# Fourth layer of a cross-attention kernel: scores in halves, two transpose banks, K and Q projected two blocks ahead

## The reference, cut to what matters

```
Q = x Wq' + bq,  K = ctx Wk' + bk,  V = ctx Wv' + bv          (256 -> 256, 16 heads of 16)
A = softmax(Q K' / 4)  per head                               (128 x 128, no mask)
y = x + (A V) Wo' + bo
out = (y - mean) / sqrt(var + 1e-5) * gamma + beta
```

## Time and profile before

| | |
|---|---|
| runs | 3356.8, 3352.99, 3349.3 us |
| profiled execution | 3355.26 us, its span 3353.6 us |
| TensorE (matmul) busy | 3019.1 us, 90% of the span |
| VectorE busy | 2043.1 us, 61% |
| ScalarE busy | 1894.9 us, 57% |
| POOL busy | 1487.5 us, 44% |
| mean granted TensorE clock | 0.959 of full speed |
| fourth layer | first exponentials at 3024 us, end at 3353.6 us |

### The profile page before, as it was taken

One profiled execution on the slowest core, in us unless ns is written; L12 is line 12 of the kernel. 1 busy time (PEld: TensorE's weight loads), 2 busy tenths in 40 slices (PEclk: granted clock), 3 DMA queues, 4 the chain that ended last, 5 costly groups with the idle time before them and its releaser, 6 DMA issues. The chain is left out here.

```text
span 3353.6 us, 82485 instructions
## 1 busy us (share of the span) xinstructions
PE 3019.1 (90%) x28656; PEld 2682.5 (80%) x28656; DVE 2043.1 (61%) x4340; ACT 1894.9 (57%) x7796; POOL 1487.5 (44%) x1874
## 2 busy tenths in 40 slices
PE   8999999689999999637999999999999999847886
PEld 6999998479999999636888888888888888746665
DVE  3445454244444444336777787788778877726775
ACT  3444444134444444326777777777777777616664
POOL 1233422103444544611555555555555555543545
PEclk9999999899999999868999999999999999978998
DMA  3112221311111110032222222333111111123331
GB/s 131 58 57 68 80 76 38 132 48 39 45 53 53 53 46 20 35 129 78 86 74 70 67 69 73 95 93 123 56 58 59 61 61 57 33 69 97 96 100 40
DMA packets 218390, 232.87 MB, mean 69 GB/s; under 512 B 41952, under 2 KB 183264, under 8 KB 215904
## 3 DMA queue, kind: packets, MB, share of 16 engines
q1 hardware_dynamic: 218208, 230.49, 21.6%
HBM read 148.57 MB, written 65.01 MB: 64 GB/s over the span
## 5 line engine op out<-in xcount | busy, mean ns | idle before, releaser
L1757 ACT ACTIVATE middle_stage<-middle_psum,middle_neg_max 128x128 f32<-128x128 f32 x2048 | 726.1, 391 | 330.4 <-DVE middle_neg_max L1737 330.2
L1757 ACT ACTIVATION_READ_ACCUMULATOR middle_stage<-middle_psum,middle_neg_max 128x1 f32 x2048 | 471.8, 230 | 0.0
L1737 DVE TENSOR_REDUCE middle_neg_max<-middle_psum 128x4 f32<-128x512 f32 x512 | 337.3, 680 | 51.2 <-PE middle_psum L1700 49.1
L1711 PE MATMUL middle_psum<-middle_eye,middle_stage 128*128 128x128 f32 x2048 | 321.5, 280 | 18.4 <-DVE middle_stage L1743 8.3
L1711 PEld LDWEIGHTS middle_psum<-middle_eye,middle_stage 128*128 128x128 f32 x2048 | 231.9, 142 | 71.8 <-issue 46.4
L1666 POOL TENSOR_TENSOR middle_attended_lo<-middle_mix,middle_attended_hi 128x256 fp32r<-128x256 f32 x128 | 94.9, 741 | 436.4 <-DVE middle_attended_hi L1749 436.4
L1757 ACT ACTIVATE fourth_stage<-fourth_psum,fourth_neg_max 128x128 f32<-128x128 f32 x512 | 182.9, 400 | 93.5 <-DVE fourth_neg_max L1737 93.4
L536 POOL TENSOR_TENSOR cross_ff_hidden_lo<-cross_ff_relu,cross_ff_hidden_hi 128x256 fp32r<-128x256 f32 x128 | 100.9, 789 | 279.7 <-DVE cross_ff_hidden_hi L531 279.7
L97 PE MATMUL middle_psum<-middle_n_yt_hi,middle_w_lo 128*128 128x256 f32 x640 | 194.1, 303 | 13.7 <-ACT middle_n_y L1874 12.1
L1967 POOL TENSOR_TENSOR middle_ff_hidden_lo<-middle_ff_relu,middle_ff_hidden_hi 128x256 fp32r<-128x256 f32 x256 | 183.5, 737 | 48.8 <-DVE middle_ff_hidden_hi L1961 48.8
L1743 DVE COPY middle_stage<-middle_psum 128x512 f32<-128x512 f32 x256 | 175.2, 684 | 16.8 <-PE middle_psum L1711 16.5
(11 more groups left out here) (351 smaller groups left out, 10910.4 us busy)
## 6 DMA issues: line engine op xcount, KB each, us to landing
middle_stage<-middle_a_k SPq DMA_DIRECT2D x1024, 16.0 KB, 1.8
middle_xt_hi<-x_hi SPq DMA_DIRECT2D x32, 256.0 KB, 2.7
middle_xt_lo<-x_lo SPq DMA_DIRECT2D x32, 256.0 KB, 3.0
middle_mask_flags<-flags SPq DMA_DIRECT2D x128, 64.0 KB, 1.9
middle_ct_hi<-context_hi SPq DMA_DIRECT2D x32, 256.0 KB, 2.9
middle_ct_lo<-context_lo SPq DMA_DIRECT2D x32, 256.0 KB, 3.1
middle_x_rows<-x_rows SPq DMA_DIRECT2D x32, 256.0 KB, 2.7
x_rows<-middle_n_z SPq DMA_DIRECT2D x32, 256.0 KB, 2.2
```

The source lines that it names most:

```text
L1711: ins = pe.transpose(banks.psum[:, TURN_BANK, x * SEQ:(x + 1) * SEQ], self.sh.p_wide[:, 4 * b + t, x, :], self.sh.eye[:])
L1737: dve.tensor_reduce(self.sh.neg_max[:, 4 * b + t, :], psum[:, SCORE_BANKS[t], :].rearrange("p (x k) -> p x k", x=4), AX_X, ALU.max, negate ...
L1757: ins = act.activation(self.sh.p_wide[:, 4 * b + t, x, :], psum[:, SCORE_BANKS[t], x * SEQ:(x + 1) * SEQ], ACT.Exp, bias=self.sh.neg_max[: ...
```

## The change

In the fourth layer alone:

- `AttendHalves` takes the place of `AttendWide`. `pe_scores` does one **half**, two of the four banks (0 and 1, or 2 and 3), and signals by itself; it claims only its two banks.
- The scores run half a step further ahead: step `here` makes scores (here,1, second half), (after,0, both halves) and (after,1, first half). The maxima move along.
- `pe_turn` and `dve_turned` alternate between banks 4 and 7; V goes through bank 6 with K, Q and the output projection.
- K and Q are both projected and evicted for block here+2. Q was projected for here+1 before. K comes at the start of the step, Q near its end.
- SP loads `x` for block here+4 behind the K copies and the residual rows, where it loaded it for here+3 ahead of them. Its store comes last, as before.
- Ahead of the loop, Q of block 1 and one and a half more scores calls are made.

POOL's order and the numbers of matmul, VectorE and ScalarE instructions per block stay the same. The diff, cut to its core:

```diff
+class AttendHalves(AttendWide):
+    visits = 2 * B2
+    turn_banks = (TURN_BANK, FF_BANK)
+    def pe_scores(self, pe, r, banks, b, half):
+        if b == 0 and half == 0:
...
+        tokens = slice(b * SEQ, (b + 1) * SEQ)
+        groups = (2 * half, 2 * half + 1)
+        banks.claim(pe, r, *(SCORE_BANKS[t] for t in groups))
+        for c in range(C):
+            for t in groups:
+                rows = slice(32 * t, 32 * t + 32)
+                ins = pe.matmul(banks.psum[:, SCORE_BANKS[t], c * T2:(c + 1) * T2].rearrange(
+                    "p (e k) -> p e k", e=2), self.proj.q[rows, c, tokens], self.proj.k_block[rows, c, :, tokens],
+                    start=True, stop=True)
+        ins.then_inc(self.scores_ready.sem, 1)
+        for t in groups:
+            banks.read(SCORE_BANKS[t], self.exp_done, 4 * b + t + 1, r=r)
+    def pe_turn(self, pe, r, banks, b, t):
+        bank = self.turn_banks[t % 2]
...
+    def dve_max(self, dve, r, psum, b, t):
+        dve.wait_ge(self.scores_ready.sem, self.scores_ready.at(r, 2 * b + t // 2 + 1))
...
 class Track:
-        self.proj = Project16(kit, f"a{i}", layer.weights_of(0), layer.stream, FF_BANK)
+        self.proj = Project16(kit, f"a{i}", layer.weights_of(0), layer.stream)
-        self.att = AttendWide(kit, f"a{i}", self.proj, [None], layer.out_of(0), layer.sh)
+        self.att = AttendHalves(kit, f"a{i}", self.proj, [None], layer.out_of(0), layer.sh)
...
 # sync, body
-                    if loaded:
-                        loaded[0].sp_x(sp, loaded[1], x, tokens(r, i, 3))
+                    queries = near(r, i, 4)
                     if keys:
                         keys[0].proj.sp_k_chunk(sp, keys[1], 0)
...
                         keys[0].sp_rows(sp, keys[1], x, tokens(r, i, 2))
+                    if queries:
+                        queries[0].sp_x(sp, queries[1], x, tokens(r, i, 4))
                     if before:
                         before[0].sp_store(sp, before[1], out, tokens(r, i, -2))
...
 # scalar, body
                     exp(here, 1, 0)
+                    exp(here, 1, 1)
+                    if keys:
+                        keys[0].proj.act_k(act, keys[1], psum)
                     if before:
                         before[0].att.act_spread(act, before[1], psum, 1)
-                    exp(here, 1, 1)
                     exp(here, 1, 2)
-                    if after:
-                        after[0].proj.act_q(act, after[1], psum)
                     exp(here, 1, 3)
                     exp(after, 0, 0)
-                    if keys:
-                        keys[0].proj.act_k(act, keys[1], psum)
                     exp(after, 0, 1)
                     if here:
                         here[0].att.act_spread(act, here[1], psum, 0)
                     exp(after, 0, 2)
+                    if keys:
+                        keys[0].proj.act_q(act, keys[1], psum)
                     exp(after, 0, 3)
...
 # vector, body, as it is after the change
                     inverse(here, 0)
                     maximum(here, 1, 2)
                     turned(here, 0, 0)
                     maximum(here, 1, 3)
                     turned(here, 0, 1)
                     norm(before, 1)
                     turned(here, 0, 2)
                     maximum(after, 0, 0)
                     maximum(after, 0, 1)
                     after[0].proj.dve_v(dve, after[1], psum)
                     turned(here, 0, 3)
                     inverse(here, 1)
                     maximum(after, 0, 2)
                     turned(here, 1, 0)
                     maximum(after, 0, 3)
                     before[0].norm.dve_sum(...)
                     turned(here, 1, 1)
                     norm(here, 0)
                     turned(here, 1, 2)
                     maximum(after, 1, 0)
                     maximum(after, 1, 1)
                     before[0].norm.dve_moments(dve, before[1])
                     turned(here, 1, 3)
...
 # tensor, body, as it is after the change
                     scores(here, 1, 1)
                     turn(here, 0, 0)
                     project_k(keys)
                     turn(here, 0, 1)
                     mix(before, 1)
                     turn(here, 0, 2)
                     scores(after, 0, 0)
                     after[0].proj.pe_v(pe, after[1], banks, after[0].ct)
                     turn(here, 0, 3)
                     scores(after, 0, 1)
                     turn(here, 1, 0)
                     before[0].att.pe_out(pe, before[1], banks, before[0].norm.sum_ready)
                     turn(here, 1, 1)
                     mix(here, 0)
                     turn(here, 1, 2)
                     scores(after, 1, 0)
                     project_q(keys)
                     turn(here, 1, 3)
```

More of the change, by code:

```diff
@@ L3051, in _ @@
             tracks[1].sp_context(sp, 0, ctx_t, tokens(0, 1, 0))
+            tracks[1].sp_x(sp, 0, x, tokens(0, 1, 0))
             sp.wait_ge(layer.block_zeroed.sem, 1)
             tracks[0].proj.sp_k(sp, 0)
-            tracks[1].sp_x(sp, 0, x, tokens(0, 1, 0))
             tracks[0].sp_context(sp, 1, ctx_t, tokens(0, 0, 2))
@@ L3059, in _ @@
                 tracks[i].sp_rows(sp, 0, x, tokens(0, i, 0))
-            tracks[0].sp_x(sp, 1, x, tokens(0, 0, 2))
+            for i in range(2):
+                tracks[i].sp_x(sp, 1, x, tokens(0, i, 2))
             run(sp, body)
@@ L3097, in _ @@
             tracks[1].proj.act_k(act, 0, psum)
+            tracks[1].proj.act_q(act, 0, psum)
             for t in range(4):
@@ L3124, in body @@
                     inverse(here, 0)
-                    maximum(here, 1, 0)
+                    maximum(here, 1, 2)
                     turned(here, 0, 0)
-                    maximum(here, 1, 1)
+                    maximum(here, 1, 3)
+                    turned(here, 0, 1)
                     norm(before, 1)
-                    turned(here, 0, 1)
-                    maximum(here, 1, 2)
-                    maximum(here, 1, 3)
                     turned(here, 0, 2)
+                    maximum(after, 0, 0)
+                    maximum(after, 0, 1)
+                    if after:
+                        after[0].proj.dve_v(dve, after[1], psum)
                     turned(here, 0, 3)
+                    inverse(here, 1)
+                    maximum(after, 0, 2)
+                    turned(here, 1, 0)
+                    maximum(after, 0, 3)
                     if before:
@@ L3137, in body @@
                                                before[0].stored)
[L3138 to L3141, removed]
                     turned(here, 1, 1)
-                    maximum(after, 0, 2)
-                    maximum(after, 0, 3)
                     norm(here, 0)
                     turned(here, 1, 2)
+                    maximum(after, 1, 0)
+                    maximum(after, 1, 1)
                     if before:
                         before[0].norm.dve_moments(dve, before[1])
-                    if after:
-                        after[0].proj.dve_v(dve, after[1], psum)
                     turned(here, 1, 3)
@@ L3169, in _ @@
                 maximum((tracks[0], 0), 0, t)
+            for t in range(2):
+                maximum((tracks[0], 0), 1, t)
             run(dve, body)
@@ L3201, in turn, with scores, mix @@
                     of[0].att.pe_turn(pe, of[1], banks, b, t)
+            def scores(of, b, half):
+                if of:
+                    of[0].att.pe_scores(pe, of[1], banks, b, half)
+            def mix(of, b):
+                if of:
+                    of[0].att.pe_mix(pe, of[1], banks, b)
             def project_k(of):
@@ L3250, in _ @@
             project_k((tracks[1], 0))
+            project_q((tracks[1], 0))
             pe.wait_ge(layer.zeroed.sem, 2)
             pe.wait_ge(layer.consts.sem, 2)
-            tracks[0].att.pe_scores(pe, 0, banks, 0)
+            scores(first, 0, 0)
+            scores(first, 0, 1)
+            scores(first, 1, 0)
             run(pe, body)
```

48 lines of the change are left out of this document (32 added, 16 removed).

## The result

The changed kernel takes **3364.65 us** (median of 6 runs, 3359.87 to 3368.21) against 3351.36 for the kernel before (6 runs, 3346.86 to 3356.8): a ratio of 1.0037, 95% interval [1.0026, 1.0047]. The changed kernel is slower by about 13 us, and the predicted range of 3328 to 3359 does not hold the time.

What follows compares the result with a forecast made beforehand. It took a serial TensorE-ScalarE loop as the bound, ScalarE's work plus waits. Loop 0.1, step 0 0.5, block 14 -2.9 and tail -6 gave -8.3: 3347.0 from 3355.26 profiled, which stood 2.3 above the median; predicted 3345, range 3328 to 3359.

Steps and rivals of the forecast that it cites:

- The clock term: In the loop, TensorE falls to 1.2 GHz in six of thirteen steps instead of five, each 1.5 us: 9.0 us.
- Rival 3: In the loop, half clock in every step behind the 1.9 us gap, 3.0 us a step: 3375 us; chance 0.12.
- Rival 1: In the loop, denser TensorE work stops the clock falling, 9.0 us goes: 3336 us; chance 0.2.
- The clean step: A full-clock loop step was to take 18.4 us against 18.3 before, so not to move.
- two exponentials 2.81: 8.06. The scores(after,0,1) need that bank: Mid-step, ScalarE's two exponentials after the first spread end at 8.06 us, and TensorE's next scores start then.
- The walk: Piece-by-piece timing of TensorE and ScalarE through the new step, from the previous step's last exponential to 18.4 us.
- Block 14's step: The step after the thirteen full ones, now without K and Q, was to take 14.9 us instead of 17.78: -2.9.
- the spread at +4.99: Early in the new step, the mix of the block before was to be readable for ScalarE's spread at 4.99 us.
- the half at 1.07: Each scores call on two banks was charged like a whole one, 1.07 us until a transpose can start.
- the 1.89 gap: At the step's end, TensorE was to be free from about 16.5 to 18.4 us, 1.9 in one piece.
- the tail: From block 15's start to the end, 39.13 us before, was to shrink by 6, between 3 and 7.5.
- Step 0: The step ahead of the thirteen, 18.84 us before, was to change by plus 0.5, between -2 and +2.

Runs made afterwards that it cites:

- fill_gap: Changed kernel with the step's last four transposes, behind the Q projection, issued four times over to fill TensorE's gap; 3345.24 us, ratio 0.9977.
- fill_elsewhere: Changed kernel with twelve more transposes per step in the middle of TensorE's dense stretch, leaving the gap; 3379.30 us, ratio 1.0088.
- store_first: Kernel before, with SP's store moved up behind the x load and ahead of the K copies; 3349.82 us, ratio 1.0001.
- old_order_pairs: Kernel before, with each four-bank scores call of the fourth layer issued as two halves back to back; 3351.85 us, ratio 1.0000.
- q_last: Changed kernel with ScalarE's Q eviction moved behind the last exponential of the step; 3320.93 us, ratio 0.9906 to the kernel before.
- before_filled: Kernel before, with twelve useless transposes more per fourth-layer step in a thin stretch of TensorE; 3349.30 us, ratio 0.9973.

## Why the prediction was wrong

**The clock term failed.** The step "I take six in thirteen instead of five, each 1.5", 9.0 in all, came out as 11 of 13, each 1.57: 17.3, or 8.3 more. The argument was that a thin stretch of the same sum of idle time brings a drop about as often, whether the idle time is in pieces or in one. Five in thirteen with 1.7 in pieces against 11 in thirteen with 1.89 in one piece do not bear that out. fill_gap (0.58, no drop) against fill_elsewhere (1.89, six) shows that the drops of the changed kernel need the gap. Those six against eleven at the same 1.89 show that how often it brings a drop depends on more than its length. Rival 3 named the right mechanism, half clock behind the 1.9 gap in nearly every step. It was priced at 3.0 a step, in the middle of 1.5 to 4.9; measured 1.57 lies at the lower bound, since TensorE was at half clock for 3.4 and back at full clock at +3.8 (3192.20). At the lower bound its sum would have been 13 x 1.5 = 19.5 in place of the 9.0: 3355.5, still short of the result by the clean step's share. Rival 1, that the drops stop, was wrong for this kernel; with the gap filled they do stop (fill_gap).

**The clean step was mis-sized: 18.82 for 18.4.** 13 x 0.42 = 5.5. The failed step is "two exponentials 2.81: 8.06. The scores(after,0,1) need that bank". The walk gave that moment to the scores as if TensorE were free. But TensorE takes its work in order: scores at +5.32, V from +6.38 (3175.94), four transposes behind it, and only then, at +8.44 (3178.00), scores(after,0,1). ScalarE's two exponentials had ended at +8.0, as the walk had them. I had followed one queue into the bank and not the other up to the same instruction. From there the remainder was right, 10.38 against 10.34.

**Block 14's step was too good.** It gained 0.97, not 2.9: there is a drop in it (clock 0.90). In fill_gap it has none and takes 15.31 against the 14.9 of the walk. The 0.4 that is left is as much as in the clean step, and the walk leaves out V ahead of scores(after,0,1) here too. (Its pieces add up to 11.6 for the second spread, where it says 11.8.)

**Ahead of step 0** nothing was priced, and 1.03 stands there. The untouched stages ended 1.80 later, inside the scatter of the profiled executions, and the way from the first matmul to step 0 is 0.77 shorter.

**Right**: the spread at +4.99; TensorE's 16.93 busy a step (17.1 said); the half at 1.07; the 1.89 gap (1.9); ScalarE's waits moved from maxima to spreads and Q, no store wait; the tail at -5.2 (-6 said, -3 to -7.5). The tail's agreement is weak, though: in the old order it took 39.1 in this profile and 37.5 and 36.1 in those of store_first and old_order_pairs, which differ from it in SP's order and in the order inside a scores call alone. Step 0 came out at -0.76, inside its bounds of -2 to +2.

Added up against the -8.3 of the prediction: clock +8.3, clean steps +5.5, block 14 +1.9, start +1.0, tail +0.8, step 0 -1.3, together 16.2. -8.3 + 16.2 = 7.9, for the 8.0 measured. The place of one ScalarE instruction decided the sign: q_last is 33 us faster than the kernel before in its series (3354.16). The prediction even named it ("the Q eviction sit on ScalarE ahead of exponentials that need neither") and went on to accept it as the step.

What stays open: what, beside the gap, decides whether a drop comes and how long it lasts (11, 12, 9 and 6 of 13 in four kernels with gaps of 1.89, 1.89, 1.45 and 1.89, in one profiled execution each), and how much of the tail is the change.

## What to carry to other kernels

Before a new order is priced, walk every queue up to the same instruction and take the later one; then look in the walk for the one gap in which an engine waits for the end of another's queue, and ask what stands ahead in that queue that nobody needs yet. Here that was one eviction, worth 44 us, more than all that the change meant to move. One idle piece of TensorE of 1.5 to 1.9 us in a loop can cost the clock as well, and a run in which it is filled with work of no use gives the clock's price alone. And when stretches of two profiles are compared, cut both at the same instruction: in the kernel before, thirteen steps cut at the other batch's scores (3039.94 to 3287.19) are 247.25 and not 248.08, a difference as large as some of those looked for.

## What the runs showed of the hardware

- Transposes without use make the kernel faster: 12 in a gap of TensorE take off 19 us (fill_gap); the same 12 elsewhere in the step add 15 (fill_elsewhere, 3379.30 against 3364.65).
- A drop in the changed kernel is short: TensorE is at 1.2 GHz from 0.4 behind the end of a 1.89 gap for 3.4 us (3188.80 to 3192.20), the three pieces in it take 1.73 for 1.13, 1.04 for 0.59 and 1.94 for 1.41, and what stands behind runs at its old lengths. In fill_elsewhere some last 6.5 (3131.50 to 3138.00) behind the same gap.
- The busy share of a step does not tell whether drops come: 0.90 with none (before_filled), 0.90 with eleven in thirteen (the changed kernel), 0.84 with five (the kernel before).
- Two scores calls on different 32-row parts of the array cost as much as one when they are back to back (16 records in 1.16 against 1.15), and 1.07 each when full-array work stands between them.
